# Reordering the one-time start of a shifted-window attention kernel on one core: load order, weight split and slab measurements

## The reference

```python
def layer(x, w_qkv, pos_emb, w_out, b_out):
    g = group_norm(x, groups=32, eps=1e-5)          # mean and variance over an image and 12 channels
    g = roll(g, (-3, -3), axis=(1, 2))
    q, k, v = split(g @ w_qkv.T, 3)                 # 384 -> 1152
    # 64 windows of 7 x 7 an image, 12 heads of 32
    dots = q @ k.T * 32 ** -0.5 + pos_emb[relative position] + mask of the rolled edge
    out = softmax(dots) @ v
    out = roll(out @ w_out.T + b_out, (3, 3), axis=(1, 2))
    return x + out
```

## Time and profile before

| | us |
|---|---|
| median of 3 runs | 4302.84 (4302.73 to 4304.71) |
| the profiled execution, device time | 4301.36 |
| its span (first to last instruction in the trace) | 4299.6 |
| TensorE busy in the span | 4151.4 |
| VectorE busy | 3717.4 |
| ScalarE busy | 2271.7 |
| GpSimd busy | 2223.2 |
| start of the span to the first scores on TensorE | 110.17 |

### The profile page before, as it was taken

One profiled execution on the slowest core, in us unless ns is written; L12 is line 12 of the kernel. 1 busy time (PEld: TensorE's weight loads), 2 busy tenths in 40 slices (PEclk: granted clock), 3 DMA queues, 4 the chain that ended last, 5 costly groups with the idle time before them and its releaser, 6 DMA issues.

```text
span 4299.6 us, 166334 instructions
## 1 busy us (share of the span) xinstructions
PE 4151.4 (97%) x65384; PEld 2982.5 (69%) x65384; DVE 3717.4 (86%) x9283; ACT 2271.7 (53%) x4225; POOL 2223.2 (52%) x1933
## 2 busy tenths in 40 slices
PE   3999999999999999999999999999999999999998
PEld 1677767777777767777677677777777777776776
DVE  5888888888888888888888888888888888888887
ACT  0555555555555555555555555555555555555554
POOL 1555555555555555555455555555555555555554
PEclk9999999999999999999999999999999999999999
DMA  4445444444444444444444444444534444444442
GB/s 125 102 111 126 106 112 117 110 114 112 113 118 106 115 120 103 113 125 106 112 116 112 113 113 111 120 110 108 123 101 113 125 105 112 117 111 113 102 105 62
DMA packets 231108, 479.07 MB, mean 111 GB/s; under 512 B 39009, under 2 KB 140898, under 8 KB 222818
## 3 DMA queue, kind: packets, MB, share of 16 engines
q1 hardware_dynamic: 230338, 468.43, 43.1%
HBM read 159.99 MB, written 77.07 MB: 55 GB/s over the span
## 4 chain that ended last, share of the span: by engine, by line
PE 65%; SPq 12%; DVE 10%; DMA 6%; ACT 4%; issue 4%; POOL 0%; DVEq 0%; ACTq 0%; POOLq 0%
PE ps_pj L1102 22%; PE ps_post L1198 12%; PE ps_pj L1098 9%; SPq L466 8%; DMA stack<-qk 6%; PE ps_post L1189 4%; PE ps_sa L1136 3%; PE ps_st L1166 3%; PE ps_pv L1182 3%; PE ps_pv L1181 2%; PE ps_pv L1180 2%; PE ps_st L1136 2%; ACT ph L681 2%; PE ps_pj L1086 2%; SPq L401 2%
## 5 line engine op out<-in xcount | busy, mean ns | idle before, releaser
L575 POOL TENSOR_TENSOR rb<-tq,cst 128x588 bf16<-128x588 bf16 x512 | 606.4, 1184 | 1698.7 <-ACT tq L668 1698.7
L607 ACT ACTIVATE qk<-ps_pj 128x392 f16<-128x392 f32 x768 | 381.9, 497 | 953.9 <-PE ps_pj L1102 947.8
L681 ACT ACTIVATE ph<-ps_st,sc 64x588 f16<-64x588 f32 x1024 | 772.2, 754 | 6.5
L1102 PE MATMUL ps_pj<-xh,wh 128*128 128x392 f16 x2304 | 765.9, 332 | 6.9 <-POOL xl L539 4.1
L1102 PE MATMUL ps_pj<-xh,wl 128*128 128x392 f16 x2304 | 765.0, 332 | 0.0
L1102 PE MATMUL ps_pj<-xl,wh 128*128 128x392 f16 x2304 | 764.8, 332 | 0.0
L878 DVE TENSOR_TENSOR qk<-ps_pj,qk 128x392 f16<-128x392 f32 x768 | 433.1, 564 | 383.7 <-ACT qk L607 377.6
L561 POOL TENSOR_TENSOR pl<-pf,ph 64x588 f16<-64x588 f32 x512 | 650.3, 1270 | 149.6 <-POOL rb L575 133.7
L547 POOL TENSOR_TENSOR xb<-xs,bout 98x384 f32<-98x384 f32 x512 | 513.8, 1004 | 107.9 <-DMA out<-xb 85.6
L966 DVE TENSOR_TENSOR pl<-pf,ph 64x588 f16<-64x588 f32 x512 | 529.0, 1033 | 0.1
L1180 PE MATMUL ps_pv<-vh,ph 128*128 128x33 f16 x6144 | 516.3, 177 | 1.6 <-DVE pl L966 1.6
(11 more groups left out here) (107 smaller groups left out, 8887.3 us busy)
## 6 DMA issues: line engine op xcount, KB each, us to landing
stack<-qk SPq DMA_DIRECT2D x1536, 147.0 KB
sx<-in_x SPq DMA_DIRECT2D x66, 1176.0 KB
xs<-in_x SPq DMA_DIRECT2D x384, 84.0 KB
out<-xb SPq DMA_DIRECT2D x384, 84.0 KB
xs<-in_x SPq DMA_DIRECT2D x384, 63.0 KB
out<-xb SPq DMA_DIRECT2D x384, 63.0 KB
xs<-in_x SPq DMA_DIRECT2D x128, 66.0 KB
out<-xb SPq DMA_DIRECT2D x128, 66.0 KB
```

Source lines behind the costliest of these rows:

```text
L575: nc.gpsimd.tensor_tensor(rb[:, :, :, :], tq[:, :, :].unsqueeze(2).broadcast_to([128, 2, HH, N]), const_of("own_head").unsqueeze(1).unsque ...
L681: e = nc.scalar.activation(ph[rows, :, w * PAD:w * PAD + N].rearrange("p (a h) n -> p a h n", a=2), ps_st[rows, :, 0:HH * N].rearrange("p ...
L1102: m = mm(ps_pj[bank][:, 0:RT].rearrange("p (w n) -> p w n", w=NW), wa[:, c, o:o + 128], xa[:, b, c, :, 0:N], **on)
```

## The change

SyncE's loads are issued as slab 0, `wnat`, slab 1, `wonat`, `cst`, `brow`. The 14 position DMAs are issued from ScalarE's queue as its first instructions, behind the same wait for GpSimd's clearing of `bn`. VectorE measures slabs 0 and 1 ahead of its wait for `s_const`. The 12 weight units go through six PSUM banks in turn: the two of `ps_pj`, `ps_post`, `ps_pv` and the two of `ps_st`; ScalarE writes the high part from PSUM with the scale as an operand, and VectorE only the low part. The measurement of image 1's slab 0 stands behind the three `x_norm` of the first row. `ROW_UNITS` has the second row's x units later.

```diff
-ROW_UNITS = [u for parts in FILL for part in parts for u in part]
+ROW_UNITS = [("q", 0), ("k", 0), ("q", 1), ("k", 1), ("q", 2), ("k", 2), ("x", 0), ("v", 0), ("x", 1), ("v", 1), ("x", 2),
+             ("v", 2), ("v", 3)]
...
+        def weight_bank(u):
+            return (ps_pj[0], ps_pj[1], ps_post, ps_pv, ps_st[:, 0, :], ps_st[:, 1, :])[u % 6]
...
         @block.sync
-            sp.dma_start(cst[:, :], const[:, :]).then_inc(s_const, 16)
-            sp.dma_start(wnat[:, :, :], w_qkv.rearrange("(a p) c -> p a c", p=128)).then_inc(s_const, 16)
-            sp.dma_start(wonat[:, :, :], w_out.rearrange("(a p) c -> p a c", p=128)).then_inc(s_const, 16)
-            sp.dma_start(brow[:, :], b_out.rearrange("(a c) -> a c", a=1)).then_inc(s_const, 16)
             slab(0, 0, 0)
+            sp.dma_start(wnat[:, :, :], w_qkv.rearrange("(a p) c -> p a c", p=128)).then_inc(s_const, 16)
             slab(0, 1, 1)
-            sp.wait_ge(s_init, 1)
-            row = 2 * WS - 1
-            for r in range(WS):
-                windows = bass.AP(pos.tensor, r * row, [[1, WS], [row, WS], [1, WS]])
-                for at in (0, 64):
-                    q = at + r * WS
-                    sp.dma_start(bn[q:q + WS, :].rearrange("p (r c) -> p r c", r=WS), windows).then_inc(s_const, 16)
+            sp.dma_start(wonat[:, :, :], w_out.rearrange("(a p) c -> p a c", p=128)).then_inc(s_const, 16)
+            sp.dma_start(cst[:, :], const[:, :]).then_inc(s_const, 16)
+            sp.dma_start(brow[:, :], b_out.rearrange("(a c) -> a c", a=1)).then_inc(s_const, 16)
...
         @block.scalar
+            act.wait_ge(s_init, 1)
+            row = 2 * WS - 1
+            for r in range(WS):
+                windows = bass.AP(pos.tensor, r * row, [[1, WS], [row, WS], [1, WS]])
+                for at in (0, 64):
+                    q = at + r * WS
+                    act.dma_start(bn[q:q + WS, :].rearrange("p (r c) -> p r c", r=WS), windows).then_inc(s_const, 16)
+            act.wait_ge(s_pre, SCALES_MADE)
+            u = 0
+            for kind in ("w", "o"):
+                for c in range(KC):
+                    for a in range(3 if kind == "w" else 1):
+                        hi_ = wh if kind == "w" else woh
+                        s = sg[:, 0:1] if kind == "w" else sg[:, 1:2]
+                        act.wait_ge(s_pj, u + 1)
+                        nc.scalar.activation(hi_[:, c, a * C:(a + 1) * C], weight_bank(u)[:, 0:C], ACT.Copy,
+                                             scale=s).then_inc(s_cast, 1)
...
         @block.vector
-            dve.wait_ge(s_slab[0], 16)
-            measure(0, range(GROUPS), True)
+            for s in range(2):
+                dve.wait_ge(s_slab[s], 16)
+                measure(s, range(GROUPS), True, s)
...
-                        dve.wait_ge(s_pj, u + 1)
-                        nc.vector.tensor_scalar(hi_[:, c, cols], ps_pj[u % 2][:, 0:C], s, None, ALU.mult).then_inc(s_cast, 1)
                         dve.wait_ge(s_cast, u + 1)
-                        nc.vector.scalar_tensor_tensor(lo_[:, c, cols], ps_pj[u % 2][:, 0:C], s, hi_[:, c, cols],
+                        nc.vector.scalar_tensor_tensor(lo_[:, c, cols], weight_bank(u)[:, 0:C], s, hi_[:, c, cols],
...
-            for s in range(1, SLABS):
+            for s in range(2, SLABS):
...
-            dve.wait_ge(s_slab[0], 16 * 3)
-            measure(0, range(GROUPS), True)
             dve.wait_ge(s_fz, FZ)
...
                 x_norm(u + 1, u % 2, c, c, 0, c)
+            dve.wait_ge(s_slab[0], 16 * 3)
+            measure(0, range(GROUPS), True)
...
         @block.tensor
-                        bank_free(u + 1)
+                        need(pe, s_pjr, u + 1 - 6)
```

More of the change, by code:

```diff
@@ L128 @@
 MEAN_STEPS, ROOT_STEPS = FZ_SPREAD - 2, FZ - FZ_SPREAD - 1
-BS_MADE, SC_MADE = 13, 17
+SCALES_MADE, BS_MADE, SC_MADE = 6, 13, 17
 LEAD = 4
@@ L598, in _ @@
         def _(act):
+            act.wait_ge(s_init, 1)
[15 more added lines that the diff above has]
+                                             scale=s).then_inc(s_cast, 1)
+                        u += 1
             def high(unit, kind, i, b, p_free, stack_sem, stack_need, bank):
@@ L1054, in _ @@
                     for a in range(3 if kind == "w" else 1):
-                        bank_free(u + 1)
+                        need(pe, s_pjr, u + 1 - 6)
                         for i in range(3):
                             src = wnat[:, 3 * a + i, :] if kind == "w" else wonat[:, i, :]
-                            m = nc.tensor.transpose(ps_pj[u % 2][:, i * 128:(i + 1) * 128], src[:, c * 128:(c + 1) * 128], ident)
+                            m = nc.tensor.transpose(weight_bank(u)[:, i * 128:(i + 1) * 128], src[:, c * 128:(c + 1) * 128], ident)
                         m.then_inc(s_pj, 1)
```

## The result

| | before | changed |
|---|---|---|
| median (lowest to highest), 6 runs each | 4303.24 (4300.35 to 4309.22) | 4286.27 (4284.13 to 4290.76) |
| the profiled execution, device time | 4301.36 | 4287.85 |
| its span | 4299.6 | 4286.0 |
| start of the span to the first scores | 110.17 | 87.80 |
| from the first scores to the end of the span | 4189.4 | 4198.2 |

The ratio of changed to before is 0.9961, with a 95% interval of 0.9949 to 0.9973. The gain is 17.0 us by these medians. The forecast was 22.4 and 4280.4, with a range up to 4286.5, so the measured median lies inside the range by 0.2, at its upper end. The last two lines of the table hold the question: the first scores come 22.4 us earlier, as forecast, but the end of this execution comes only 13.6 earlier.

What follows compares the result with a forecast made beforehand. TensorE bounds the loop, so only its start, set by a mostly VectorE-bound chain, can move. Terms 0.9 + 7.7 + 6.5 + 4.7 + 1.3 + 1.35 = 22.4 give 4302.84 - 22.4 = 4280.4, range 4276 to 4286.5.

Steps and rivals of the forecast that it cites:

- the table load: ScalarE's table load leaves the place behind the first normalization: gain 1.3, or 1.4 more if a drain exists.
- The slower rival: Each position issue on ScalarE takes 3.85, positions land at 61.1, time 4318.5; chance 0.02.
- The rival of late slabs: SyncE's row loads delay the requests for slabs 2 and 3; 4.8 lost, 4285.2; chance 0.07.
- three signs of being wrong: High parts over 0.54 apart, VectorE waiting for a slab after the weights, lead at first scores not lead at end.
- the cost of the positions: Position DMAs on ScalarE's queue delay slab 1 by 0 to 2.7; 1.0 taken as nearest.
- loads: Reordered loads start VectorE's first reduction at 23.0 instead of 23.87: gain 0.9, between 1.9 and -0.8.
- full price: Positions hold up slab 1 for the full 2.7: reduction at 24.7, time 4282.1; chance 0.18.
- The weight units: High parts leave VectorE, 12 units take 6.5 instead of 14.15: gain 7.7, or 6.7 at 0.62 each.
- The later slabs and the statistics: Only slabs 2 and 3 left behind the weights, without waits: gain 6.5; `x_norm` directly behind the statistics: gain 4.7.
- the moved measurement: Measurement of image 1's slab 0 moves into VectorE's wait for the first q unit: gain 4.7.
- The clock rival: TensorE's shorter wait at the first scores keeps its clock at 2.4 GHz: 4279.7; chance 0.15.
- the order of the units: Unit k2 starts ahead of x0 in the first row, at 95.13 instead of 96.48: gain 1.35.

Runs made afterwards that it cites:

- a_old_slab: Changed kernel with the measurement of image 1's slab 0 back ahead of the first normalization; median 4288.93, ratio 0.9962 to the kernel before.
- a_early_reduce: Changed kernel with `wnat` on its own semaphore and reduced on VectorE between slabs 0 and 1; median 4283.74, ratio 0.9947 to the kernel before.
- a_again: Changed kernel run again without an edit; median 4283.73, ratio 0.9954 to the kernel before.
- a_third: Changed kernel run a third time without an edit; median 4281.95, ratio 0.9947 to the kernel before.
- a_two_banks: Changed kernel with the weight units in the two old banks, high parts still on ScalarE; median 4291.69, ratio 0.9969 to the kernel before.
- a_old_weights: Changed kernel with weight units as before: two banks, high and low parts both on VectorE; median 4295.43, ratio 0.9975 to the kernel before.
- a_old_order: Changed kernel with the old `ROW_UNITS` order of the first row's units; median 4287.95, ratio 0.9959 to the kernel before.
- b_new_order: Kernel before with only the new `ROW_UNITS` order; median 4301.10, ratio 0.9991 to the kernel before.
- a_pos_sync: Changed kernel with the 14 position DMAs back on SyncE's queue behind `brow`; median 4284.52, ratio 0.9952 to the kernel before.
- a_delay: Changed kernel with six extra weight reductions on VectorE delaying the start; median 4307.98, ratio 1.0009 to the kernel before.
- b_again: Kernel before run again without an edit; median 4303.69, ratio 1.0003.

## Why the prediction was right, and where it was off

**The mechanism held.** The first scores were forecast at 87.7 and stood at 87.80, and nearly all of it came by the steps named: the reduction released by VectorE's own measurement, low parts some 0.53 apart, no wait at the later slabs, the table load out of the way, the measurement in the wait for the first q unit. That the two agree within 0.1 is luck in part: in this execution the weights gave 0.8 more than forecast, and the loads and the row's units 0.3 and 0.5 less. The slower rival (3.85 an issue on ScalarE) fell at once: 14 issues took 7.45, or 0.53 each. The rival of late slabs fell too, but with little to spare: 0.39 of waiting in a_old_slab, 2.57 in a_early_reduce. Two of the prediction's three signs of being wrong did show. The lead at the first scores is not the lead at the end (see below). And ScalarE's second six high parts are 0.64 apart and not 0.54, because each waits for TensorE's transposes, which are 0.64 apart. This cost nothing, since the low parts stayed 0.53 apart behind them.

**What was off most is the cost of the positions,** put at "about a third, 1.0" between 0 and 2.7. They cost slab 1 2.3 in the mean of eight executions, near the full price. Together with the kernel before's own first reduction (23.87 and 23.55), the term "loads" is not a gain of 0.9 but a loss of 0.6 in the eight (24.3 against 23.7), and of 0.2 in the changed kernel's own three (23.29, 24.04, 24.43). The windows of the changed kernel show that the low share in the earlier trace rows was the wrong measure:

```profile
3.00:12.00 9.00, 0.00 (x0) 0.00 (x0) 4.09 (x28) 0.00 (x0) 8.74 (x7) 1.00 1.05 308
17.40:21.00 3.60, 0.00 (x0) 0.00 (x0) 2.44 (x17) 0.00 (x0) 0.00 (x0) 1.00 1.03 368
```

```profile
q10 hardware_dynamic: 784, 0.02, 0.0%
```

The DMA engines are full until 21, and the positions are 784 packets for 0.02 MB on a queue of their own (last line, from the page: packets, MB, share). The share of 0.35 before was taken when the bulk loads were over and only the positions and the first row loads (84 KB and less) were in flight, so it didn't tell what the small pieces take from a full load. The rule of the Trainium skill that the prediction weighed ("DMA: Bandwidth & Descriptors", Queues, rings and completion order) was the better guide: the engines serve the rings in turn, so the positions get ahead of slab 1. The runs agree in direction, with 19.5 against 17.23, and the rival "full price", 4282.1, is nearer to the truth than the forecast. The prediction priced slab 1 alone; the early weights of a_early_reduce were held up by 4.1 or more.

**The weight units were worth as much as forecast or a little more:** 7.8 in a_again and a_third (15.91 against 8.14 and 8.15), 8.5 in the first trace (against 7.36), and 7.7 was forecast. The 12 low parts are as forecast. What differs between the three is TensorE's clock. In the first trace it is granted in full until 42.3, its product for the output bias (1x384) takes 0.88, and `bout` waits 0.63 for it. In the other two it is at half from 31.2 and 31.0 on, the same product takes 1.59, and `bout` waits longer:

```profile
42.90 0.56 DVE L792 COPY bout<-ps_pj 98x384 f32<-98x384 f32 x1 [1.16 <-PE ps_pj L1082]
```

The prediction took the banks for granted, as what lets ScalarE keep ahead. a_two_banks prices them: ScalarE's work is 1.8 of the gain, and without the six banks the rest doesn't come.

**The later slabs and the statistics:** no wait in three executions, as forecast, and the moved measurement gave the 4.7. For the table load the prediction weighed 1.4 more by the page "ScalarE: Activation LUTs" of the Trainium skill (What ACT_TABLE_LOAD costs), for a drain. No run here shows it: the lead grows from 20.2 at `x_norm` to 21.5 at the first projection, by 1.3, which is the load of 1.28 alone, and a_old_weights, which puts the load back, loses 1.29 there.

**The clock rival came true in one trace of three.** In the first one TensorE waited 2.05 for the first scores, and the clock behind them stayed at 2.4 GHz, where the earlier trace rows show half of it:

```profile
88.30:91.00 2.70, 2.02 (x13) 1.00 (x14) 2.53 (x6) 0.63 (x2) 0.32 (x1) 1.00 0.23 75
```

GpSimd's first loop instruction there leads by 23.4, 1.0 more than the scores. In a_again and a_third TensorE waited 2.06, and the clock fell to half at 89.3 and 89.0, some 1 us behind the first scores (88.23 and 88.30). The projections of a_third stand 0.32 apart there, where they stand 0.17 apart in the first trace:

```profile
89.14 0.53 PE L1116 MATMUL ps_pj<-xl,wh 128*128 128x392 f16 x1
89.46 0.53 PE L1116 MATMUL ps_pj<-xh,wh 128*128 128x392 f16 x1
```

GpSimd's first loop instruction comes 3.4 behind the scores in the first trace, 3.8 and 4.1 in these two, and 4.4 in the kernel before. So 0.3 to 1.0 of lead came of it at that place.

**Sum at the first scores:** by three executions of the changed kernel (87.80, 88.23, 88.30) and two of the kernel before, the lead is 109.8 - 88.1 = 21.7. The terms as these five traces show them are -0.2 for the loads, 8.0 weights, 6.3 slabs, 4.7 measurement, 1.3 table load, and 1.7 from first projection to first scores: 21.8.

**The end.** The gain there is 19.9 (standard error 0.9), so 2.5 less than the forecast. Of these, 0.7 are missing at the first scores already. Whether the other 1.8 are lost in the loop is open, and the records don't agree:

- By the times of all executions it is little. In the table's last column the eleven kernels of the changed family have a mean of 4195.9, and the three of the old one 4193.3. But the latter are only three, and one of them isn't the kernel before. The 60 executions of the kernel before in the four groups have a mean of 4304.8, which less 109.8 is 4195.0. The eleven kernels' means less their first scores are 4195.8 on average. The difference is 0.8, with a standard error of 0.7.
- By the traces alone it is more. From first scores to end of span the three old ones took 4187.2 to 4190.3, and the eleven changed ones 4188.2 to 4198.2, mean 4194.3. But the three executions traced were 1.9 to 3.7 faster than the medians of their kernels.

No part of the change can be named as the cause. By the last column, none that was undone alone takes the loss away: order 4197.4, weights 4197.4, measurement 4195.9, positions 4197.2. By the traces, a_old_order has the shortest stretch of the family (4188.2), but its traced execution was 4 to 8.5 us faster than its four others. What was seen is that the stretch follows the waits for the stack DMAs: they sum to 16.0 in b_new_order and 15.9 in a_old_order, the two shortest, and to 25.0 and 26.3 in the first trace and a_pos_sync, the two longest (4198.2). Why these waits are longer in one execution than in another was not found, and they aren't all: at some 21, the kernel before took 4189.4 and 4190.3, a_third 4193.9. Half of the 8.8 of the first trace didn't come back: it was 3.5 to 4.5 in the next two (4193.8 and 4193.9 from scores to end of span, against 4189.4 and 4190.3 in the kernel before).

## What to carry to other kernels

When work is moved to another DMA queue, price it by what is in flight beside it and not by the share that it had when alone: many small pieces on a second queue held up a bulk load by nearly all the time that they had taken at its end (2.3 of 2.7), and the weights ahead of it by at least 4.1, in one pair of traces. When a second engine takes half of a step, count the buffers too, since here the six banks gave 6.7 of 8.5 us in the best case and the second engine 1.8. When a run undoes one part, ask what else it undoes: putting the weights back on VectorE also brought ScalarE's table load back. And where a program scatters by 3 us from run to run, read a saving of 20 at the place where it is made, and repeat the comparison before a rest of 5 at the end is given a cause.

## What the runs showed of the hardware that was not expected

- 14 DMAs of 49 pieces each were issued from ScalarE's idle queue in 7.16 to 9.07 us, 0.51 to 0.65 each, and from SyncE's behind the bulk loads in 12.07 to 12.64, 0.86 to 0.90 each.
- In the changed kernel's first trace TensorE's granted clock was at half (1.2 GHz) from 42.3 us on, when TensorE did little work (0.61 of 13 us in the first row), and with the first row's projections it stayed there until some 69, though TensorE was busy all the time from 66 on (second row). In a_again and a_third it was at half from 31 on. The same holds, from 31 to 44 on, for the other kernels with six banks except a_delay. In the kernel before, b_again, b_new_order, a_two_banks, a_old_weights and a_delay the records have the full clock until the first scores, with idle stretches like these (0.47 of the 10 us from 50 on, before). But the first projections stand 0.33 apart there as well, and 0.17 apart only later (from 90.0 on before, 4.8 behind the first one). So for such a stretch the distance of the matmuls tells more than the granted clock. In the changed kernel the first projections at full clock come at 69.5, 5.8 behind the first one, and in a_third at 68.5, 2.9 behind it. From first projection to first scores it took 24.1, 23.0 and 22.7 in its three executions, a spread of 1.4, as large as the whole gain from the order of the units.

```profile
42.00:55.00 13.00, 0.61 (x2) 0.50 (x2) 12.07 (x70) 0.00 (x0) 0.00 (x0) 0.51 0.57 160
...
66.00:70.00 4.00, 4.00 (x15) 1.82 (x14) 1.09 (x5) 0.75 (x2) 0.00 (x0) 0.55 0.01 4
```

- A wait of 3.4 us ahead of the first scores was followed by half of the clock in all three traces that have it (before, b_again, a_old_order). One of 2.05 to 2.12 was followed by half of the clock in six traces of eleven, among them two of the changed kernel's three, and by the full clock in five.
- The stretch from the first scores to the end of the span, with the same instructions, took 4193.8, 4193.9 and 4198.2 in three executions of the changed kernel. Single runs of it went from 4279.51 to 4290.76.
